# Feed-forward weights in fp4: four roundings from DVE to GpSimd, the turn one group earlier, its copies on ScalarE

## The reference

```
def fp4_quant_dequant(x):              # blocks of 16 along the last dim
    scale = max(|block|) / 6, at least 1e-12
    xn = block / scale
    idx = searchsorted([.25,.75,1.25,1.75,2.5,3.5,5], |xn|)
    return GRID[idx] * sign(xn) * scale     # GRID = 0,.5,1,1.5,2,3,4,6
gate = fp4(x) @ fp4(w_gate).T          # w_gate, w_up: 352 x 128
h = silu(gate) * (fp4(x) @ fp4(w_up).T)
f = fp4(h) @ fp4(w_down).T             # w_down: 128 x 352
```

## Time and profile before

| | us |
|---|---|
| runs, median of three | 825.81 (822.59 to 826.52) |
| profiled execution, its own time | 824.34 |
| its span in the profile | 822.6 |
| projections, first to last instruction | about 13.2 to 132.6 |
| first instruction after their barrier | 133.57 |
| DVE, POOL, ScalarE, TensorE busy in one loop turn of 12.5 | 11.76, 4.91, 8.20, 8.02 |

### The profile page before, as it was taken

The page is one execution under the profiler, slowest core; times in us unless marked ns, Lnnn a source line. Parts: engine busy times, 40 slices in busy tenths (PEclk is TensorE's granted clock), DMA queues, the critical chain, the costliest instruction groups (busy, mean ns, idle before and its releaser), DMA issues. The chain is left out here.

```text
span 822.6 us, 14081 instructions
## 1 busy us (share of the span) xinstructions
PE 629.0 (76%) x4241; PEld 324.2 (39%) x4242; DVE 589.5 (72%) x1424; ACT 480.6 (58%) x828; POOL 356.2 (43%) x506
## 2 busy tenths in 40 slices
PE   1366555999999999999999728877759877998920
PEld 1244332333333333333333216656536544654510
DVE  3899996779797979797977676797625443586734
ACT  2356665899999999999999512223324333444430
POOL 0234353234343434344433211117635777666653
PEclk9776865999999999999999956868759999999965
DMA  4200005940000000000000040012112222334241
GB/s 120 75 14 26 26 1 109 153 94 27 26 25 25 25 25 25 25 25 25 25 27 2 1 154 26 26 32 72 51 50 71 74 77 64 107 89 127 67 134 51
DMA packets 52978, 45.31 MB, mean 55 GB/s; under 512 B 5936, under 2 KB 47216, under 8 KB 52688
## 3 DMA queue, kind: packets, MB, share of 16 engines
q1 hardware_dynamic: 45600, 34.97, 16.5%
q0 software_dynamic: 4544, 9.35, 3.3%
q10 hardware_dynamic: 2800, 0.58, 0.3%
HBM read 15.72 MB, written 16.59 MB: 39 GB/s over the span
## 5 line engine op out<-in xcount | busy, mean ns | idle before, releaser
L733 ACT ACTIVATE attend_prob<-attend_ring 128x1024 f32<-128x1024 f32 (+1 forms) x320 | 280.0, 951 | 17.0 <-PE attend_ring L859 15.0
L682 POOL TENSOR_SCALAR_AFFINE_SELECT attend_prob<-attend_prob 128x256 f32<-128x256 f32 x256 | 117.2, 481 | 144.2 <-ACT attend_prob L733 143.9
L879 PE MATMUL attend_ps_o<-attend_prob,attend_v_slot 128*32 128x512 f32 (+3 forms) x1536 | 157.3, 498 | 0.0
L859 PE MATMUL attend_ring<-attend_qk_slot 32*128 32x512 f16 (+3 forms) x768 | 93.0, 334 | 15.5 <-ACT attend_prob L733 8.8
L1604 POOL DMA_INDIRECT expert_outputs<-expert_y_out,expert_goal_now x78 | 77.1, 988 | 53.1 <-POOL expert_goal_now L1599 20.3
L1790 PE MATMUL expert_ps_h<-w,expert_x_t 128*128 x156 | 89.9, 660 | 0.5 <-ACT expert_x_t L1724 0.5
L1737 ACT ACTIVATE expert_tanh<-expert_ps_h 128x256 f32<-128x256 f32 x78 | 30.0, 385 | 95.2 <-PE expert_ps_h L1790 95.2
L947 POOL DMA_INDIRECT slots<-rows,slot_index x64 | 61.5, 962 | 41.0 <-issue 41.0
L859 PEld LDWEIGHTS attend_ring<-attend_qk_slot 32*128 32x128 f16 x768 | 25.8, 91 | 130.5 <-ACT attend_prob L733 45.5
L1812 PE MATMUL expert_ps_y<-w,expert_hidden_t 128*128 x312 | 53.2, 294 | 14.4 <-DVE expert_y_out L1662 13.5
L1646 DVE SCALAR_TENSOR_TENSOR expert_silu<-expert_tanh,expert_ps_h 128x256 f32<-128x256 f32 x78 | 32.7, 419 | 42.6 <-ACT expert_tanh L1737 42.5
(11 more groups left out here) (235 smaller groups left out, 1223.0 us busy)
## 6 DMA issues: line engine op xcount, KB each, us to landing
attend_qk_slot<-qk_parts SPq DMA_DIRECT2D x16, 512.0 KB, 2.9
slots<-attend_zeros SPq DMA_DIRECT2D x26, 193.5 KB, 9.5
x_pairs<-slots SPq DMA_DIRECT2D x26, 193.5 KB, 2.6
expert_y_in<-expert_outputs SPq DMA_DIRECT2D x8, 512.0 KB, 4.8
xn_all<-project_xn SPq DMA_DIRECT2D x8, 256.0 KB, 2.3
w<-w_laid SPq DMA_DIRECT2D x1, 2048.0 KB, 7.7
rows<-rows SPq DMA_DIRECT2D x4, 512.0 KB, 3.6
out<-expert_result SPq DMA_DIRECT2D x8, 256.0 KB, 2.4
```

The costliest lines, as they stand in the source:

```text
L682: ins = nc.gpsimd.affine_select(out=edge, in_=edge, compare_op=ALU.is_ge, fill=0.0, base=0, pattern=[[0, 2], [1, P]], channel_multiplier=-1)
L733: nc.scalar.activation(probs(k, pair)[:, :, 0:width], scores[:, :, 0:width], ACT.Exp, scale=HD ** -0.5).then_inc(exp_made[u][pair], 1)
L859: ins = nc.tensor.matmul(dst[:, s * QC + at:s * QC + at + cols], qk_slot[slot][rows, T + j * P:T + (j + 1) * P], qk_slot[slot][rows, qc * ...
L879: ins = nc.tensor.matmul(ps_o[RB * s:RB * (s + 1), off:QC], v4[slot][:, j, s], probs(k, s // 2)[:, s % 2, at:at + cols], start=j == 0, sto ...
```

## The change

The first three parts of the rounding stay on DVE. The last four leave DVE and `after(7)`. Five plain steps on GpSimd take their place (`round_weights`): ratio*ratio; power*slope + base; power + ratio; power - ratio; ratio*scale. The first is issued behind turn -1 (no other work of GpSimd's comes before it in the phase), the second and third behind turn 0, the fourth behind turn 5, the fifth behind turn 6. TensorE turns the matrices behind turn 7 and ahead of turn 8, and ScalarE, also behind turn 7, copies them out of PSUM. The sizes and the arithmetic are the same.

```diff
--- before.py
+++ after.py
@@ -219,8 +219,8 @@
         fp4_power, fp4_ratio = sb("fp4_power", FP4), sb("fp4_ratio", FP4)
         fp4_amax, fp4_scale, fp4_inverse = (sb(f"fp4_{n}", FP4 // BLK) for n in ("amax", "scale", "inverse"))
         ps_w = bank("ps_w")
-        fp4_step = [sem(f"fp4_step{i}") for i in range(8)]
-        w_turned, w_kept = sem("w_turned"), sem("w_kept")
+        fp4_step = [sem(f"fp4_step{i}") for i in range(7)]
+        w_rounded, w_turned, w_kept = sem("w_rounded"), sem("w_turned"), sem("w_kept")
         x_in, fp4_in = [sem(f"x_in{b}") for b in range(1, BATCH)], sem("fp4_in")
 
 
@@ -350,18 +350,6 @@
                     dve.wait_ge(fp4_in, 16 * 7)
                     for n in range(3):
                         ins = fp4_part(nc, dve, n, m.fp4_nat, fp4_buf, fp4_ratio, 1e-12, fp4_step, 1)
-                if u == GROUPS - 1:
-                    for n in range(3, FP4_PARTS):
-                        ins = fp4_part(nc, dve, n, m.fp4_nat, fp4_buf, fp4_ratio, 1e-12, fp4_step, 1)
-                    ins.then_inc(fp4_step[7], 1)
-                    for j in range(len(jobs)):
-                        dve.wait_ge(w_turned, j + 1)
-                        if j < len(w_dst):
-                            ins = nc.vector.tensor_copy(w_dst[j], ps_w[:, 0:INNER])
-                        else:
-                            for i, (_, r) in enumerate(ICH):
-                                ins = nc.vector.tensor_copy(m.down_w[0:r, i * P:(i + 1) * P], ps_w[0:r, i * P:(i + 1) * P])
-                        ins.then_inc(w_kept, 1)
 
             fp4_buf = fp4_amax, fp4_scale, fp4_inverse, fp4_power
             run(dve, body, after)
@@ -396,7 +384,30 @@
                     nc.gpsimd.tensor_tensor(part[odd][1][:, :, 1::2], bcast(rot_h[1], 2, 2), part[odd][1][:, :, 0::2],
                                             ALU.subtract).then_inc(k_low, 1)
 
-            run(pool, body)
+            def round_weights(n):
+
+                if n == 0:
+                    pool.wait_ge(fp4_step[2], 1)
+                else:
+                    pool.wait_ge(w_rounded, n)
+                blocks = lambda x: x.rearrange("p (b k) -> p b k", k=BLK)
+                if n == 0:
+                    ins = nc.gpsimd.tensor_tensor(fp4_power, fp4_ratio, fp4_ratio, ALU.mult)
+                elif n == 1:
+                    ins = nc.gpsimd.tensor_scalar(fp4_power, fp4_power, FP4_SLOPE, FP4_BASE, ALU.mult, ALU.add)
+                elif n == 2:
+                    ins = nc.gpsimd.tensor_tensor(fp4_ratio, fp4_power, fp4_ratio, ALU.add)
+                elif n == 3:
+                    ins = nc.gpsimd.tensor_tensor(fp4_ratio, fp4_power, fp4_ratio, ALU.subtract)
+                else:
+                    ins = nc.gpsimd.tensor_tensor(blocks(fp4_ratio), blocks(fp4_ratio), bcast(fp4_scale, 2, BLK), ALU.mult)
+                ins.then_inc(w_rounded, 1)
+
+            def after(u):
+                for n in {-1: (0,), 0: (1, 2), GROUPS - 3: (3,), GROUPS - 2: (4,)}.get(u, ()):
+                    round_weights(n)
+
+            run(pool, body, after)
 
         @block.scalar
         def _(act):
@@ -447,7 +458,19 @@
                     for q in range(2, QUADS):
                         keep(d, q)
 
-            run(act, body)
+            def after(u):
+                if u != GROUPS - 1:
+                    return
+                for j in range(len(jobs)):
+                    act.wait_ge(w_turned, j + 1)
+                    if j < len(w_dst):
+                        ins = nc.scalar.activation(w_dst[j], ps_w[:, 0:INNER], ACT.Copy)
+                    else:
+                        for i, (_, r) in enumerate(ICH):
+                            ins = nc.scalar.activation(m.down_w[0:r, i * P:(i + 1) * P], ps_w[0:r, i * P:(i + 1) * P], ACT.Copy)
+                    ins.then_inc(w_kept, 1)
+
+            run(act, body, after)
 
         @block.tensor
         def _(pe):
@@ -491,9 +514,9 @@
                     turn_quads(d, range(2, QUADS))
 
             def after(u):
-                if u < GROUPS:
+                if u != GROUPS - 1:
                     return
-                pe.wait_ge(fp4_step[7], 1)
+                pe.wait_ge(w_rounded, 5)
                 for j in range(len(jobs)):
                     once(pe, w_kept, j)
                     at = 0
```

## The result

The changed kernel takes 829.99 us (median of 7 runs, 828.99 to 832.17) beside 825.81 of the kernel before on the same chip: ratio 1.0064, interval 1.0044 to 1.0084. It was compared twice more: 1.0099 (1.0080 to 1.0117) and 1.0100 (1.0072 to 1.0128). A ratio is estimated from all runs of both kernels; in the first comparison it makes 5.3 us, where the two medians differ by 4.2. The first two comparisons ran where the kernel before takes about 825 us, as experiments 5 to 8 did; the third, and experiments 1 to 4, 9, 11 and 12, ran where it takes 855 to 859. Ratios are always to runs of the kernel before in the same session.

A forecast was written before the change was run, and what follows sets the result against it. DVE's queue was taken to bound the projections. Turns costing 2.4 + 2.4 + 4.3 = 9.1 us plus 0.1 at the end give 9.2: 833.6 from 824.34, 835.0 from the median; forecast 834.0, range 828 to 838.5.

The forecast's parts named there:

- What bounds the phase: Projections: DVE's in-order queue is the path, busy 11.76 of a 12.50 us turn; whatever delays it is not regained.
- One at a time: Around the sine products, two-input DVE and SBUF-reading GpSimd instructions exclude each other: turns cost 9.1 us, without exclusion 1.8.
- Rival A: No exclusion for the new GpSimd instructions, only GpSimd's own queue delays the sines: 826.2 us, chance 0.14.
- Prices: The new GpSimd steps: 2.15 us for each of four two-input steps, 1.35 for the one with constants.
- The scale's 0.5: Turn 0: DVE's 70-column scale no longer waits for the sine, so the cosine can start 0.5 us sooner.
- The end: End of projections: weight work moves from DVE's end ahead of group 7's quads, two nearly equal chains, plus 0.1 us.
- From the phase to the time: After the projections: all 9.2 us reach the execution time, the later phases taking as long as before.
- B: ScalarE fits the copies into its waits and the turns cost nothing: 822.2 us, chance 0.05.
- C: GpSimd's steps cost the high ends of their prices, with 1 us more at the end: 837.2 us, chance 0.13.
- D: GpSimd's first use of a new instruction kind costs extra: near 840 us, chance 0.03.

The follow-up runs named there:

- experiment 5: The changed kernel again, no edit, against the kernel before: 831.85 us beside 824.24, ratio 1.0099.
- experiment 6: Changed kernel with the five steps in GpSimd's waits and ScalarE keeping group 6's quads ahead of group 7's halves: 820.84 us, before 824.24, ratio 0.9960.
- experiment 7: Changed kernel with only the end undone (TensorE turns behind turn 8, DVE copies as before): 830.96 us, before 824.24, ratio 1.0088.
- experiment 8: The kernel before, padded with three more DVE instructions at the end of the projections: 829.11 us beside 824.24, ratio 1.0040.
- experiment 1: The kernel before, padded with seven more DVE instructions at the end of the projections: 868.32 us beside 859.47, ratio 1.0088.
- experiment 2: Changed kernel without GpSimd's five rounding steps, weights left unrounded: 858.23 us, kernel before 859.47, ratio 0.9983.
- experiment 3: Changed kernel with the GpSimd steps replaced by about equally long memsets that read nothing, weights unrounded: 858.92 us, kernel before 859.47, ratio 0.9988.
- experiment 4: Changed kernel with the same five steps moved into GpSimd's waits for ScalarE's half of k: 858.87 us, kernel before 859.47, ratio 0.9997.
- experiment 9: The kernel before against itself: 856.23 us beside 855.43, ratio 1.0012.
- experiment 11: Second run of the changed kernel with its five steps moved into GpSimd's waits: 857.68 us, kernel before 855.43, ratio 1.0020.
- experiment 12: Second run of the kernel with steps in GpSimd's waits and group 6's quads ahead of group 7's halves: 853.34 us, before 856.48, ratio 0.9957.

## Why the prediction held, point by point

The forecast was 834.0 in 828 to 838.5, slower; the measured median is 829.99, slower. The forecast is 8.2 us over the median before; the three comparisons came to 5.3, 8.2 and 8.6 by their ratios. In the projections the mechanism is the one predicted. From rotation to rotation, predicted and measured in the first trace after:

| step | before | after | cost | predicted |
|---|---|---|---|---|
| L337 of group 0 to rotation 0 | 7.56 | 9.74 | 2.2 | 2.4 |
| to rotation 1 | 12.39 | 14.97 | 2.6 | 2.4 |
| to rotation 5 | 50.18 | 50.22 | 0 | 0 |
| to rotation 6 | 11.29 | 13.76 | 2.5 | 2.15 |
| to rotation 7 | 10.24 | 12.11 | 1.9 | 2.15 |
| to the attention | 15.98 | 15.84 | -0.1 | 0.1 |
| sum | 107.64 | 116.64 | 9.0 | 9.2 |

- **What bounds the phase: right.** Turns 2 to 5, untouched, take the same time; every us that a rotation was late came through.
- **One at a time: right.** The ends of the trains follow one another as worked out, and experiment 3 shows that the exclusion, not the queue, is the larger part. Rival A's 1.9 us is what the memsets cost, 1.9 in the interval. The Trainium skill's rule in "SBUF — State Buffer" ("Who interferes with whom") also says that a GpSimd instruction that only writes does not meet DVE's two-input one; the trace of experiment 3 agrees (1.21 us beside a memset).
- **Prices: right in sum.** Behind what held them, the two-input steps took 1.91, 2.42, 2.41 and 1.96 us (predicted 2.15 each), the constants 0.98 (1.35): 9.7 against 9.95. The bare or scaled product is cheaper, the sums with two different inputs dearer.
- **The scale's 0.5: right.** It took 0.20 us against 0.78. The experiments whose sine went back ahead of it (2 and 4) have 0.78 again.
- **The end: right in sum, for two reasons instead of one.** I had it as two chains of equal length. They are equal because 1.3 us won and 1.3 lost cancel (experiment 7), and how fast TensorE's clock let it turn the weights is in both. The wait for the second copy was longer than worked out (0.94 us against 0.62) because that turn took 0.85 us and not the 0.52 that I had read at the high clock; the last quads were quicker (3.81 against 4.10).
- **From the phase to the time: the term that was mis-sized.** I carried 9.2 us through at full size and expected the time from the attention's first instruction to the end to be as before; it was 689.0 us before and 686.4 after, and 7.3 us arrived in the mean of the three comparisons. Where the rest went is open. The kernels with more instructions on POOL have a linear stretch 1.8 us shorter in almost all traces, and 9.0 - 1.8 = 7.2 would fit. But the two padded kernels, whose stretch is as long as before, deliver no larger share (7.6 of 9.9, 3.3 of 4.2; their intervals just allow all of it), and the kernel of experiments 4 and 11, whose stretch is short, is not under the kernel before. So the fit may be luck.
- **Rivals.** A (826.2), B (822.2), C (837.2) and D are out, by the trace more than by the time, which at 829.99 lies between A and the forecast: the cosines are stretched, the rotations late, the prices are not at their high ends, and the first constant step on POOL took 0.98 us behind what held it.

## What to carry to other kernels

Before moving elementwise work from DVE to POOL, list which of DVE's instructions have two inputs in SBUF and put POOL's work beside the others (reductions, reciprocals, PSUM sources): the same five instructions cost 9.0 us in one place and 0.9 in another. Idle time of an engine is only worth something where the next thing in its queue is not already awaited; a step goes in front of a wait, not behind it. And where an engine's work leaves the end of a phase, look for what ends second: here nothing was gained until four quads were moved into ScalarE's wait as well.

## What the runs showed of the hardware that was not expected

Five more instructions on POOL in one phase go with a stretch of another phase, some 390 us later, that is shorter by 1.4 to 2.8 us in nine traces of nine; the memsets of experiment 3 do it as well as real work. What differs there is when TensorE's granted clock is low: 0.50 during sixteen matmuls that DVE waits for in the kernel before, 1.00 during them in the changed kernel. That this reaches the time of a run is not shown. And the spread between two comparisons of the same pair of kernels (1.0064, 1.0099, 1.0100) is as wide as the stated intervals.
